# Transformer block on one core: the softmax denominator's blocks move from TensorE to GpSimd, with four buffers of P

## The reference, cut to what matters

```python
# x: [4, 2048, 512] f32; 16 heads of 32; weights 512 x 512
def attn(x):                       # causal, and every 4th key column masked
    q, k, v = heads(x @ Wq + bq), heads(x @ Wk + bk), heads(x @ Wv + bv)
    att = einsum('bhtd,bhsd->bhts', q, k) / sqrt(32)
    att = where(mask == 0, -inf, att);  att = softmax(att)
    return merge(einsum('bhts,bhsd->bhtd', att, v)) @ Wp + bp
def ffn(x):                        # one of 8 experts, chosen from logits and u
    i = argmax(log_softmax(logits) - log(-log(u)))
    return x @ W[i] + b[i]
x = x + layernorm(attn(layernorm(x)))
x = x + layernorm(ffn(layernorm(x)))
```

## Time and profile before

| | |
|---|---|
| runs | 2433.01, 2435.17, 2436.12 us |
| profiled execution | 2434.55 us, span 2432.6 us |
| mean granted clock | 0.987 |
| TensorE, VectorE, ScalarE, GpSimd busy | 95%, 69%, 71%, 58% |
| exps (ScalarE L949) | 1920, 1073.1 us |
| adds of GpSimd (L817) | 546, 682.3 us |
| sum matmuls (L1318) | 2688 records, 285.1 us |

### The profile page before, as it was taken

One profiled execution on the slowest core, in us unless ns is written; L12 is line 12 of the kernel. 1 busy time (PEld: TensorE's weight loads), 2 busy tenths in 40 slices (PEclk: granted clock), 3 DMA queues, 4 the chain that ended last, 5 costly groups with the idle time before them and its releaser, 6 DMA issues.

```text
span 2432.6 us, 43804 instructions
## 1 busy us (share of the span) xinstructions
PE 2321.4 (95%) x15380; PEld 966.1 (40%) x15380; DVE 1686.6 (69%) x4832; ACT 1719.4 (71%) x3142; POOL 1408.3 (58%) x1318
## 2 busy tenths in 40 slices
PE   4899999999999999999999999999899999999996
PEld 2444443433454443433344443343334444334322
DVE  7867677676477678677466867777728676777774
ACT  6667676777777667677776867767767676776673
POOL 2245465685655457477854637657765455665734
PEclk9899999999999999999999999999999999999998
DMA  7213131121233113022132313102114231301001
GB/s 197 67 42 93 28 78 35 41 55 41 50 89 78 57 43 80 17 51 51 33 87 59 92 31 75 48 23 58 38 46 94 60 80 31 83 22 40 30 1 35
DMA packets 224357, 137.50 MB, mean 57 GB/s; under 512 B 146730, under 2 KB 196618, under 8 KB 224138
## 3 DMA queue, kind: packets, MB, share of 16 engines
q1 hardware_dynamic: 222310, 134.65, 22.1%
q10 hardware_dynamic: 1828, 0.07, 0.1%
HBM read 39.69 MB, written 16.78 MB: 23 GB/s over the span
## 4 chain that ended last, share of the span: by engine, by line
PE 74%; DVE 10%; ACT 6%; issue 5%; POOL 5%; DMA 1%; SPq 0%; POOLq 0%; ACTq 0%; DVEq 0%
PE acc L1303 13%; PE acc L1267 12%; PE acc L1287 11%; PE acc L1238 9%; PE acc L1239 9%; PE acc L1240 9%; PE acc L1318 8%; ACT P L949 4%; POOL P L817 3%; DVE acc L1042 2%; PE acc L1291 2%; DVE MP L1046 2%; DVE MHL L1057 1%; PE acc L1243 1%; DVE STA L1015 1%
## 5 line engine op out<-in xcount | busy, mean ns | idle before, releaser
L949 ACT ACTIVATE P<-acc,EX 128x512 f32<-128x512 f32 (+2 forms) x1920 | 1073.1, 641 | 314.5 <-PE acc L1291 153.9
L1046 DVE TENSOR_REDUCE MP<-acc 128x1 f32<-128x512 f32 (+1 forms) x1088 | 720.6, 679 | 254.2 <-PE acc L1267 250.7
L817 POOL TENSOR_TENSOR P<-P 128x512 f32<-128x512 f32 x546 | 682.3, 1280 | 84.1 <-PE acc L1303 48.8
L1267 PE MATMUL acc<-KST,QST 96*128 96x512 f16 (+10 forms) x2112 | 593.2, 334 | 27.5 <-DVE MP L1046 11.9
L1042 DVE CUSTOM_DVE_ANT_0 acc<-acc,CB 128x96 f32<-128x96 f32 (+7 forms) x1024 | 449.5, 455 | 211.3 <-PE acc L1267 207.7
L1287 PE MATMUL acc<-QST,KST 98*128 98x512 f16 (+2 forms) x1920 | 579.1, 355 | 16.6 <-DVE MP L1046 5.7
L1303 PE MATMUL acc<-P,V 128*32 128x512 f32 (+2 forms) x3840 | 443.1, 546 | 3.6 <-ACT P L949 2.9
L1267 PEld LDWEIGHTS acc<-KST,QST 96*128 96x128 f16 x2112 | 194.9, 98 | 335.9 <-issue 60.2
L1287 PEld LDWEIGHTS acc<-QST,KST 98*128 98x128 f16 x1920 | 182.9, 98 | 294.7 <-issue 71.5
L1318 PE MATMUL acc<-P,ONES 128*32 128x512 f32 (+2 forms) x2688 | 285.1, 517 | 2.0 <-ACT P L949 1.9
L796 POOL TENSOR_TENSOR RR<-RR,NHALF 128x1 f32<-128x1 f32 x256 | 141.9, 557 | 236.8 <-DVE NM L1020 236.0
(11 more groups left out here) (144 smaller groups left out, 2983.8 us busy)
## 6 DMA issues: line engine op xcount, KB each, us to landing
QST<-QKH SPq DMA_DIRECT2D x128, 128.0 KB, 3.2
XR<-in_L_attn_x_dram SPq DMA_DIRECT2D x60, 256.0 KB, 2.8
out_dram<-XR SPq DMA_DIRECT2D x60, 256.0 KB, 2.1
KST<-QKH SPq DMA_DIRECT2D x128, 96.0 KB, 2.7
XB<-in_L_attn_x_dram SPq DMA_DIRECT2D x48, 252.0 KB
QST<-QKL SPq DMA_DIRECT2D x64, 128.0 KB, 3.3
KST<-QKL SPq DMA_DIRECT2D x64, 96.0 KB, 2.7
XB<-in_L_attn_x_dram SPq DMA_DIRECT2D x20, 256.0 KB, 3.3
```

The lines of the kernel that those rows point to most:

```text
L817: e.tensor_tensor(P[:, acc, a, :], P[:, acc, a, :], P[:, buf, a, :], ALU.add).then_inc(g_s, 1)
L949: e.activation(P[:, p_buf[u, g, sb_], a, t0:512], bank(*step)[:, t0:512], ACT.Exp, scale=EX[:, 1:2]).then_inc(a_e, 1)
L1046: e.tensor_reduce(maxima(u, g)[:, r, a, ci:ci + 1], bank(*s)[:, 0:n], AX.X, ALU.max).then_inc(v_m, 1)
L1267: i = e.matmul(bank(*s)[:, 0:n], QST[0:96, h, 128 * r:128 * r + 128], KST[0:96, h, c0:c0 + n], start=True, stop=True)
```

## The change

- `on_pe` keeps only the diagonal blocks: all whole blocks below the diagonal but block 0 are added by GpSimd (by VectorE where the last unit has it so), and TensorE sums the accumulator and the three diagonal blocks.
- P has four buffers, one accumulator and a ring of three; `p_blocks` hands them out, and the accumulator's buffer goes to the end of the ring after its group.
- `high` is done by ScalarE (an ACTIVATE with Copy) instead of VectorE.
- `out` on ScalarE and `scale` on GpSimd are gone; one VectorE instruction (`scalar_tensor_tensor`, from PSUM, times the scale, times the inverses) writes SC tile 1 after `invert`. The PSUM bank of pv is freed by it.
- For the room, V holds four units instead of five and YX three tiles instead of four. The v projections of a new sequence's unit wait for the pv blocks of the last unit of the sequence before that read the same place; row n's p projection waits for `add_y` of row n-3, and the very last row uses a tile of XR. Constants and biases that lay in V's spare part lie in YX and in V's unit 3.
- The planner tries 4 windows (20, 30, 45 and 60 us) with 6 plans each.

```diff
 def on_pe(j, sb):
-    return sb >= 3 * j or sb % 3 == 1
+    return sb >= 3 * j
...
 def p_blocks(NB, NJ):
 
     buf, first, before, held = {}, {}, {}, {}
-    last, acc = 2, 0
+    ring = [0, 1, 2, 3]
     for u in range(NB * NJ):
         for g in range(4):
-            new = [i for i in range(3) if i not in (acc, last)][0]
-            ring = [last, acc]
-            acc = first[u, g] = new
             for sb in range(3 * (u % NJ) + 3):
-                last = acc if sb == 0 else ring[(sb - 1) % 2]
-                buf[u, g, sb] = last
-                if last in held:
-                    before[u, g, sb] = held[last]
-                held[last] = u, g, sb
+                now = buf[u, g, sb] = ring.pop(0)
+                if sb:
+                    ring.append(now)
+                else:
+                    first[u, g] = now
+                if now in held:
+                    before[u, g, sb] = held[now]
+                held[now] = u, g, sb
+            ring.append(first[u, g])
     return buf, first, before
...
-    ROUNDS, WINDOW = 5, 20000
+    ROUNDS, WINDOWS = 6, (20000, 30000, 45000, 60000)
...
-                add("dve", at, 400 if which == "k" else 470, ("high", job), [("act", "evac", job)], [("QKH", ("sp", "spread", job))])
-                add("gp", at, 870 if which == "k" else 1110, ("rest", job), [("dve", "high", job)])
+                add("act", at, 420 if which == "k" else 540, ("high", job), [("act", "evac", job)], [("QKH", ("sp", "spread", job))])
+                add("gp", at, 870 if which == "k" else 1110, ("rest", job), [("act", "high", job)])
                 add("sp", at, 1950, ("spread", job), [("gp", "rest", job)])
...
-            old = u - 2
             self.project(("v", u, a), self.place(s, -self.V + 6 * a), 512, 590, turned + [("dve", "wlow", 2)]
-                         + [("dve", "fold", 2)] * (u > 0) + ([("pe", "pv", old, 3, 3 * (old % NJ) + 2)] if u > 1 else []))
+                         + [("dve", "fold", 2)] * (u > 0) + ([("pe", "pv", u // NJ * NJ - 1, 3, 3 * j + 2)] if u >= NJ else []))
...
-                    [] if sb else [("psO", ("act", "out", u, g))])
+                    [] if sb else [("psO", ("dve", "out", u, g))])
...
-            add("act", s + 0.95, 570, ("out", u, g), [("pe", "pv", u, g, last)], [("SC", ("gp", "olow", u, g))])
-            add("dve", s + 0.95, 1600, ("invert", u, g), [("pe", "sum", u, g, last)]
-                + [("gp", "scale", *divmod(s - 1, 4))] * (s > 0))
-            add("gp", s + 1.1, 1225, ("scale", u, g), [("dve", "invert", u, g), ("act", "out", u, g)])
-            add("act", s + 1.1, 540, ("ohigh", u, g), [("gp", "scale", u, g)]
+            add("dve", s + 0.95, 1600, ("invert", u, g), [("pe", "sum", u, g, last)])
+            add("dve", s + 0.95, 610, ("out", u, g), [("dve", "invert", u, g), ("pe", "pv", u, g, last)],
+                [("SC", ("gp", "olow", u, g))])
+            add("act", s + 1.1, 540, ("ohigh", u, g), [("dve", "out", u, g)]
                 + [("pe", "proj", ("p", u - 1, r), 3) for r in range(4) if u])
             add("gp", s + 1.1, 1112, ("olow", u, g), [("act", "ohigh", u, g)])
...
-                         + ([("gp", "add_y", u - 1, r)] if u else []))
+                         + ([("sp", "store", *divmod(n - 6, 4))] if n == 4 * self.NU - 1 else
+                            [("gp", "add_y", *divmod(n - 3, 4))] if n > 2 else []))
...
-        V = sb("V", [128, 3 * (NJ + 1), 512], F32)
+        V = sb("V", [128, 3 * NJ, 512], F32)
...
-        P = sb("P", [128, 3, 4, 512], F32)
+        P = sb("P", [128, 4, 4, 512], F32)
...
-        YX = sb("YX", [128, 4, 512], F32)
+        YX = sb("YX", [128, 3, 512], F32)
...
+        def yx(u, r):
+
+            n = 4 * u + r
+            return YX[:, n % 3, :] if n < 4 * NU - 1 else XR[:, 0, :]
...
-                elif kind == "scale":
-                    u, g = s[1:]
-                    gp.wait_ge(v_o, DV["invert", u, g])
-                    gp.wait_ge(a_o, AC["out", u, g])
-                    e.tensor_tensor(SC[:, 1, :], SC[:, 1, :], SC[:, 0, :], ALU.mult).then_inc(g_o, 1)
...
-                        if u > 1:
-                            ac.wait_ge(p_pv, PE["pv", u - 2, 3, 3 * ((u - 2) % NJ) + 2])
-                        e.activation(V[:, 3 * (u % (NJ + 1)) + i, :], ps, ACT.Copy, scale=CO[:, 2:3]).then_inc(a_v, 1)
+                        if u >= NJ:
+                            ac.wait_ge(p_pv, PE["pv", u // NJ * NJ - 1, 3, 3 * (u % NJ) + 2])
+                        e.activation(V[:, 3 * (u % NJ) + i, :], ps, ACT.Copy, scale=CO[:, 2:3]).then_inc(a_v, 1)
                     elif name == "p":
-                        if u:
-                            ac.wait_ge(g_r, GP["add_y", u - 1, i])
-                        e.activation(YX[:, i, :], ps, ACT.Copy, scale=CO[:, 3:4]).then_inc(a_y, 1)
+                        n = 4 * u + i
+                        if n == 4 * NU - 1:
+                            ac.wait_ge(d_o[0], 16 * len(range(0, 4 * NU - 4, 3)))
+                        elif n > 2:
+                            ac.wait_ge(g_r, GP["add_y", *divmod(n - 3, 4)])
+                        e.activation(yx(u, i), ps, ACT.Copy, scale=CO[:, 3:4]).then_inc(a_y, 1)
                     else:
                         ac.wait_ge(g_p, GP["low", 2, u, i])
                         e.activation(resid(u, i), ps, ACT.Copy, scale=CO[:, 4:5]).then_inc(a_y, 1)
+                elif kind == "high":
+                    job = s[1]
...
+                    at, n = q_slot[job], 384 if job[0] == "k" else 512
+                    ac.wait_ge(a_q, AC["evac", job])
+                    if at > 1:
+                        was, wu, wm = q_job[at - 2]
+                        ac.wait_ge(d_qk[was][wm], 48 * (wu + 1))
+                    e.activation(QKH[:, at % 2, 0:n], SC[:, 2, 0:n], ACT.Copy).then_inc(a_h, 1)
...
-                elif kind == "out":
-                    u, g = s[1:]
-                    n = 4 * u + g
-                    if n:
-                        ac.wait_ge(g_o, GP["olow", *divmod(n - 1, 4)])
-                    ac.wait_ge(p_pv, PE["pv", u, g, 3 * (u % NJ) + 2])
-                    e.activation(SC[:, 1, :], bank("pv", u, g, 0), ACT.Copy, scale=SS[:, 2:3]).then_inc(a_o, 1)
...
+                elif kind == "out":
+                    u, g = s[1:]
+                    n = 4 * u + g
+                    dv.wait_ge(p_pv, PE["pv", u, g, 3 * (u % NJ) + 2])
+                    dv.wait_ge(v_o, DV["invert", u, g])
+                    if n:
+                        dv.wait_ge(g_o, GP["olow", *divmod(n - 1, 4)])
+                    e.scalar_tensor_tensor(out=SC[:, 1, :], in0=bank("pv", u, g, 0), scalar=SS[:, 2:3], in1=SC[:, 0, :],
+                                           op0=ALU.mult, op1=ALU.mult).then_inc(v_t, 1)
...
-                    vb = 3 * ((u - j + sb_ // 3) % (NJ + 1)) + sb_ % 3
+                    vb = sb_
```

More of the change, by code:

```diff
@@ L92, in __init__ @@
                 self.users[n].append(key)
[L93 to L99, removed]
+        plans = []
+        for window in self.WINDOWS:
+            self.rank = {key: step[0] for key, step in self.steps.items()}
+            for _ in range(self.ROUNDS):
+                plans.append(self.run())
+                self.rank = self.backwards(window)
+                if self.rank is None:
+                    break
         _, lists, self.bank, self.emptier, self.times = min(plans, key=lambda plan: plan[0])
@@ L399, in offer @@
         def offer(key):
-            if late[key] - self.WINDOW > now:
-                events.append((late[key] - self.WINDOW, "offer", key))
+            if late[key] - window > now:
+                events.append((late[key] - window, "offer", key))
                 return
@@ L597, in sandwich_block @@
                                             "whigh": ("w", 4 if s[0] == "whigh" and s[1] < 2 else 1), "exp": ("e", 1),
-                                            "out": ("o", 1), "ohigh": ("o", 1), "shift": ("m", 1), "cast": ("c", 1), "norm": ("n", 2)}[s[0]]))
+                                            "ohigh": ("o", 1), "shift": ("m", 1), "high": ("h", 1), "cast": ("c", 1), "norm": ("n", 2)}[s[0]]))
         DV = counted(order.dve, lambda s: {
@@ L602, in sandwich_block @@
             "fold": ("f", 17 if s[-1] == 2 else 1), "stats": ("ln", 4), "norm": ("n", 1),
-            "high": ("q", 1), "peak": ("m", 1), "peaks": ("m", 3), "add": ("s", 1), "invert": ("o", 3)}[s[0]])
+            "peak": ("m", 1), "peaks": ("m", 3), "add": ("s", 1), "invert": ("o", 3), "out": ("t", 1)}[s[0]])
         GP = counted(order.gp, lambda s: {
             "rstd": ("ln", 1), "low": ("p", 1), "rest": ("q", 1), "add": ("s", 1),
-            "scale": ("o", 1), "olow": ("o", 1), "add_x": ("r", 1), "add_y": ("r", 1)}[s[0]])
+            "olow": ("o", 1), "add_x": ("r", 1), "add_y": ("r", 1)}[s[0]])
         staged = max(DV[s] for s in (("wlow", 0, 3), ("wlow", 1, 3), ("wlow", 2)))
```

(18 more changed lines are left out.)

35 lines of the change are left out of this document (18 added, 17 removed).

## The result

| | before | after |
|---|---|---|
| median | 2434.39 us | 2560.46 us (2558.12 to 2561.01) |
| ratio | | 1.0509, 95% interval 1.0492 to 1.0526 |
| span of the profiled execution | 2432.6 | 2559.2 |
| mean granted clock | 0.987 | 0.955 |

What follows compares the result with a forecast made beforehand. TensorE was taken to set the pace everywhere, with GpSimd next in the j=3 units. 2434.55 less 82.6 gave 2352.0; +19, +4, +3 and -0.6 made 2377, in round figures 2378 us, range 2348 to 2422.

Steps and rivals of the forecast that it cites:

- the shared access to SBUF: VectorE's and GpSimd's two-input SBUF adds delay each other; the new `out` never delayed, or all 64, 68 us of VectorE time.
- the finishing of a head group: The chain after a group, now `invert`, VectorE `out`, `ohigh`, `olow`: 0.6 us gained at the program's end, elsewhere nothing.
- TensorE's work: Sums of blocks 1, 4 and 7 below the diagonal leave TensorE: 96 blocks at 0.86 us, 82.6 us less.
- +19: First three j=3 units: GpSimd's adds make each 16 us longer than TensorE needs, 47 in all, 60% recovered by other work.
- +4: Last unit, group 1: GpSimd needs 44 us against 40.1, with no later work to bring in.
- +3: YX with three tiles: row 3 of a unit waits for row 0's add_y, three times after a j=3 unit; ends 0 and 33.
- -0.6: Program's end: the bare finishing chain gets 0.6 us shorter, ends +0.5 to -0.6.
- The j=3 units: Fourth 512-token units of a sequence, 12 key blocks per head group: GpSimd fills groups 1 to 3 to 95%; 210 us.
- GpSimd bounds: Rival: GpSimd bounds the j=3 units and nothing is recovered by other work; 2406 us, up to 2425; 19%.
- TensorE falls to half clock: Rival: waits for P's ring in j=3 groups drop TensorE's clock, 45 drops of 1.7 us; slower, 2455 us; 9%.
- GpSimd is hidden: Rival: the planner brings enough other work into the j=3 groups to cover GpSimd; 2352 to 2358 us; 25%.

Runs made afterwards that it cites:

- the probe: Separate program, not the kernel: VectorE instructions issued beside unbroken rows of 12 GpSimd adds; three kinds waited one add or the row's rest, 11 us, three times in nine.
- a break in four adds: The changed kernel in its own order, with every fourth GpSimd add (head 0's) waiting for the add just before it: 2384.06 us, ratio 0.9794 to the kernel before.

## Why the prediction was wrong

**The step that failed** is the one on the shared access to SBUF, under the finishing of a head group: the question was put only to the instruction that the change adds and to VectorE's adds of the last unit, "Either leaves VectorE under 75%, so the sum stays". VectorE did stay under 75% (73%), and the mean share was the wrong thing to ask for. Which of VectorE's existing instructions wait for GpSimd, and what is queued behind them, was not asked, and each wait was priced at one GpSimd instruction (1.06 us). The row to ask for was there: L1057 at 7125 ns where 174 is enough. The change makes the rows of adds longer and more frequent (28 without a gap around the longest wait, where the earlier trace rows has 16), and a VectorE instruction can wait for the whole rest of a row. By GpSimd's timelines, stretches of over 10 us without a visible hole make up 681 us of the kernel before and 1294 of the changed one. Length alone doesn't set the wait: the kernel before has rows of 16 adds and no wait for MHL over 7.1 us, and whether an instruction waits for the row or for one add is open, as in the probe. Sum of the wait: 216 us in L1055, 175 of them gone from MHL's two instructions with a break in four adds, which makes the kernel 176 us faster.

**What held.** With the break the kernel takes 2384.06 us, 6 over the 2378 forecast. Its terms:
- TensorE's work: 2253.5 us busy, 68 less than 2321.4; 82.6 less was forecast.
- TensorE's idle time: 127.4 us, 16 more than the 111.2 before; the terms +19, +4, +3 and -0.6 make 25.
- GpSimd: 1783.4 us; 1779 forecast.
- The j=3 units: 201.3, 200.6 and 200.3 us, together 12 over what TensorE alone was to need. The forecast had them 16 each over that, 210 us in the first, filled in part with work of other units. GpSimd's 96% of the whole unit is above the 95% that I gave it in three groups of four.
- `out` on VectorE: 740 to 752 ns, never delayed, 0.70 taken. `high` on ScalarE: 633 and 529 ns, 0.66 and 0.55 taken.

That agreement is between the forecast and another kernel than the one forecast, and part of it is luck: the first two terms miss by 15 and 9 us in opposite directions. The forecast for the change itself was 182 us off and on the wrong side. The working of the prediction adds up but for 0.1 us in one term (205.3 - 10.3 is 195.0, not 195.1) and a total of 2377 that became 2378.

**The rivals.** "GpSimd bounds" was the nearest by its stage and wrong by its mechanism: GpSimd was 80% busy in j=3. "TensorE falls to half clock" gave the right sign and saw a small part: half clock costs 19 us against the kernel with the break. And the idle time that brings it comes from MHL, not from waits for the ring of P, which came to 26.1 us in all; with the break the clock is 0.986. "GpSimd is hidden" comes near only once the break is in, with 12 us over TensorE's need in j=3. Other work didn't fill TensorE's idle time: in the wait shown, the next instruction of its order needed a bank that VectorE had to empty, and VectorE stood still.

## What to carry to other kernels

Before more work goes to GpSimd, list VectorE's instructions that read SBUF the way a wait was seen here (two SBUF inputs, copies, tensor_scalar over several columns), look at the longest of each, not the mean, and ask who waits for it; then compare the length of GpSimd's unbroken rows, and the share of the time that they fill, before and after. A wait of 16 us counts in full where other engines' next instructions stand behind it, as here. A wait on GpSimd's own preceding instruction was a cheap cure here, and one in four adds was better than one in two or one in one; giving the instruction a PSUM input is another that the probe points to, which wasn't tried in the block.

## What the runs showed of the hardware

- An unbroken row of GpSimd adds held a 128x16 VectorE instruction off for up to 16.31 us, thirteen adds and a subtraction; it went on 0.03 us after the row's end.
- A wait of GpSimd for its own last instruction stretches the spacing of 128x512 adds from 1.22 or 1.23 us to 1.34 in the probes and 1.41 in the block, and lets VectorE in: with it at every add neither of the two instructions that write MHL took over 1.26 us.
- In unbroken rows of the same kind, the same 128x16 instruction at nearly the same place waited 0.3 or 11.3 us; what decides is open.
- Of 230 us at half clock only a part cost time, since TensorE was idle in much of it: 19 us more busy time than at a mean clock of 0.986.
